# A relational graph layer on one core: three buffers for relation rows and one-hots, types brought in by transfers, and gathers that wait for their ring's slots

## The reference

```python
src, dst = (edge_index[0], edge_index[1])
m = x[src] * rel[edge_type]
m = jnp.concatenate([m[:half] @ W_in, m[half:] @ W_out], 0)
deg = jax.ops.segment_sum(jnp.ones((e,), x.dtype), dst, num_segments=n)
norm = 1.0 / jnp.maximum(deg, 1.0)
agg = jax.ops.segment_sum(m * norm[dst][:, None], dst, num_segments=n)
return jnp.tanh(agg + x @ W_loop + b)
```

## Time and profile before

| | |
|---|---|
| median of 3 runs | 2801.2 us (2800.81 to 2801.85) |
| span of the profiled execution | 3183.3 us |
| PE, PEld busy | 2759.1 us, 2587.3 us |
| DVE, ACT, POOL busy | 2303.9 us, 1865.5 us, 1952.0 us |
| granted TensorE clock, mean | 0.963 |
| moved by DMA | 312.57 MB |

### The profile page before, as it was taken

How to read it: one execution, slowest core, us unless ns; L and a number is a source line. 1 busy time by engine, 2 the same in 40 slices (tenths; PEclk the granted TensorE clock), 3 DMA queues, 4 the chain that set the end, 5 groups by cost and what they waited for, 6 DMA issues and landing times. The chain is left out here.

```text
span 3183.3 us, 55393 instructions
## 1 busy us (share of the span) xinstructions
PE 2759.1 (87%) x20688; PEld 2587.3 (81%) x20688; DVE 2303.9 (72%) x3258; ACT 1865.5 (59%) x3179; POOL 1952.0 (61%) x2129
## 2 busy tenths in 40 slices
PE   4888888888888888797888888888888887997998
PEld 3888888888888888796877887878777786997998
DVE  6777777777677777896777777777777776995665
ACT  6556665555555555585555555555555554785444
POOL 6666666666666666455666666666666664892223
PEclk9999989999999999899999999999999999998999
DMA  8333333333333333353333333333333333452221
GB/s 259 119 90 89 89 89 90 89 89 90 88 89 90 90 88 90 92 164 104 90 90 90 89 90 92 88 90 90 89 89 92 88 90 98 136 158 90 69 67 64
DMA packets 162458, 312.57 MB, mean 98 GB/s; under 512 B 34061, under 2 KB 95309, under 8 KB 162229
## 3 DMA queue, kind: packets, MB, share of 16 engines
q0 software_dynamic: 79872, 218.21, 23.8%
q1 hardware_dynamic: 81120, 89.89, 8.8%
q10 hardware_dynamic: 1237, 1.41, 0.2%
HBM read 263.90 MB, written 45.48 MB: 97 GB/s over the span
## 5 line engine op out<-in xcount | busy, mean ns | idle before, releaser
L740 PE MATMUL edge_rg<-edge_rel_hi,edge_hot 128*128 128x256 f32 x6656 | 1551.7, 293 | 86.6 <-issue 63.0
L740 PE MATMUL edge_rg<-edge_rel_lo,edge_hot 128*128 128x256 f32 x4992 | 1312.3, 289 | 60.0 <-issue 58.9
L740 PEld LDWEIGHTS edge_rg<-edge_rel_hi,edge_hot 128*128 128x128 f32 x6656 | 1219.6, 197 | 143.7 <-issue 92.2
L548 ACT ACTIVATE edge_hot<-edge_typ,minus_type 128x512 fp32r<-128x512 f32 x832 | 526.8, 685 | 935.9 <-DMA dense_prev<-emb_t 383.9
L740 PEld LDWEIGHTS edge_rg<-edge_rel_lo,edge_hot 128*128 128x128 f32 x4992 | 983.1, 197 | 70.0 <-issue 68.5
L623 DVE TENSOR_TENSOR edge_m_lo<-edge_rg,edge_m_hi 128x1024 fp32r<-128x1024 f32 x416 | 509.3, 1224 | 241.3 <-ACT edge_m_hi L541 127.7
L604 DVE TENSOR_SCALAR edge_hot<-edge_typ,type_of 128x512 fp32r<-128x512 f32 x832 | 582.3, 741 | 12.4 <-ACT edge_hot L548 8.7
L753 PE MATMUL edge_small<-edge_m_hi,edge_sel 128*128 128x258 f32 x1664 | 458.1, 306 | 96.3 <-DVE edge_m_lo L623 90.7
L530 POOL DMA_INDIRECT edge_xg<-emb,src x416 | 399.0, 959 | 225.9 <-issue 96.2
L530 POOL DMA_INDIRECT work<-h,src x416 | 400.7, 963 | 221.9 <-issue 101.9
L530 POOL DMA_INDIRECT edge_xg<-h,src x416 | 400.2, 962 | 216.2 <-issue 102.8
(11 more groups left out here) (183 smaller groups left out, 3933.9 us busy)
## 6 DMA issues: line engine op xcount, KB each, us to landing
work<-emb,src POOLq DMA_INDIRECT x416
edge_xg<-emb,src POOLq DMA_INDIRECT x416
work<-h,src POOLq DMA_INDIRECT x416
edge_xg<-h,src POOLq DMA_INDIRECT x416
set_x_rows<-in_x SPq DMA_DIRECT2D x25, 256.0 KB, 3.9
emb<-set_e_rows SPq DMA_DIRECT2D x25, 256.0 KB, 2.9
emb_t<-acc SPq DMA_DIRECT2D x5, 1280.0 KB
dense_prev<-emb_t SPq DMA_DIRECT2D x25, 256.0 KB, 2.7
```

Source lines behind the costliest of these rows:

```text
L548: act.activation(hot[:, q % 2, c], typ[q % 2][:], ACT.Abs, bias=K["minus_type"][:, c:c + 1]).then_inc(distances, 1)
L740: ins = pe.matmul(rg[q % 2][:, t, :], hot[:, q % 2, c, t * P:(t + 1) * P], part[:, c, :], start=(c == 0 and part is rel_hi), stop=(c == FULL))
```

## The change

- **Relation rows and one-hots have three buffers** (`DEPTH`, `of_three`), not two; `typ` in PSUM is given up for the third `rg`. The lists are new. DVE: message(3), one_window(3), low(3), add_window(6), one_hot(0). PE: one_window(3), relation_rows(0), and the transposes of four groups before stand in the middle of relation_rows. ACT: high(3), copy_sums(5), distance(0), one_hot(0), clear(3).
- **Types as int16 by transfers.** Setup writes the types as int16 to DRAM; SP starts two transfers a group (`load_types`): 512 types to all 128 partitions, and 128 types of each of the four tiles to a strip of 32 partitions. PE's spread matmul is gone. `dst` and `dst_rel` are int16 too.
- **The last types in strips.** The 16 last relations stand in each strip of 32 partitions (high part, low part). One one-hot of 128 elements a partition (`hot_rest`) serves the four tiles of a group; each tile has its own right side in `rel_rest`, zero outside its strip. The matmuls stay 28 a group.
- **Gathers** of group g wait for the message of group g - 4, once for four tiles.
- The copy of the node columns to DRAM is started from ACT, not SP. ACT's `high` waits for window sums of an earlier group, and the first window sums of a pair wait for the adds of the pair that held the same buffer.
- Preparation: eight transfers for the last relations (two before), some small operations more in setup and at the start of a layer; a buffer of zeros becomes one column.

```diff
+DEPTH = 3
+STRIP = P // GROUP
@@ phase_setup @@
             act.wait_ge(dst_in, 16)
+            act.copy(dst[:], dst_i[:]).then_inc(tables, 1)
             act.copy(K["dst"][:], dst_i[:]).then_inc(tables, 1)
             act.wait_ge(types_in, 16)
-            act.copy(K["typ"][0:TYPE_ROWS], types_i[0:TYPE_ROWS]).then_inc(tables, 1)
+            act.copy(types_h[0:TYPE_ROWS], types_i[0:TYPE_ROWS]).then_inc(tables, 1)
+            act.wait_ge(tables, 3)
+            act.dma_start(types_16.rearrange("(p k) -> p k", p=TYPE_ROWS), types_h[0:TYPE_ROWS]).then_inc(types_out, 16)
@@ phase_edges @@
-        hot = s.sb("hot", [P, 2, RCHUNKS, GROUP * P], F32R)
+        rel_rest = s.sb("rel_rest", [P, GROUP, DIM], F32R)
+        typ = s.sb("typ", [P, 2, GROUP * P], I16)
+        strips = s.sb("strips", [P, 2, P], I16)
+        hot = s.sb("hot", [P, DEPTH, FULL, GROUP * P], F32R)
+        hot_rest = s.sb("hot_rest", [P, DEPTH, P], F32R)
-        rg = [s.ps(f"rg{b}", [P, GROUP, DIM]) for b in range(2)]
-        typ = [s.ps(f"typ{b}", [P, GROUP * P]) for b in range(2)]
+        rg = [s.ps(f"rg{b}", [P, GROUP, DIM]) for b in range(DEPTH)]
@@ SP @@
+            def load_types(g):
+                wait_past(sp, hot_done, g - 1)
+                wait_past(sp, distances, HOT_ACT * (g - 1))
+                of_group = types[g * GROUP * P:(g + 1) * GROUP * P]
+                sp.dma_start(typ[:, g % 2], of_group.partition_broadcast(P)).then_inc(types_in[g % 2], 16)
+                sp.dma_start(strips[:, g % 2],
+                             of_group.rearrange("(t e) -> t e", t=GROUP).unsqueeze(1).to_broadcast([GROUP, STRIP, P]))\
+                    .then_inc(types_in[g % 2], 16)
@@ POOL @@
+                wait_past(pool, messages, g - 3)
                 for t in range(GROUP):
-
-                    if t < GROUP - 1:
-                        wait_past(pool, rel_tile, (GROUP - 1) * (g - 2) + t + 1)
-                    else:
-                        wait_past(pool, rel_done, g - 1)
@@ ACT @@
+                    act.wait_ge(messages, g + 1)
+                    if slot is of_three:
+                        wait_past(act, summed, g - 1)
-                over_groups(act, (0, later(distance)), (2, high), (0, later(one_hot)), (3, copy_sums), (0, clear_one))
+                over_groups(act, (3, high(of_three)), (5, copy_sums), (0, later(distance(of_three))),
+                            (0, later(one_hot(of_three))), (3, clear_one))
@@ DVE @@
-                for c in range(HOT_ACT, RCHUNKS):
-                    ins = dve.tensor_scalar(hot[:, q % 2, c], typ[q % 2][:], K["type_of"][:, c:c + 1], None,
-                                            ALU.is_equal)
+                    for c in range(HOT_ACT, FULL):
+                        dve.tensor_scalar(hot[:, slot(g, q), c], typ[:, q % 2], K["type_of"][:, c:c + 1], None,
+                                          ALU.is_equal)
+                    dve.tensor_scalar(hot_rest[:, slot(g, q)], strips[:, q % 2], K["type_of"][:, FULL:], None,
+                                      ALU.is_equal).then_inc(hot_done, 1)
-                over_groups(dve, (2, message), (2, one_window), (4, add_window), (2, low), (0, one_hot_later))
+                over_groups(dve, (3, message(of_three)), (3, one_window), (3, low(of_three)), (6, add_window),
+                            (0, later(one_hot(of_three))))
@@ PE @@
+                    for t in range(GROUP):
+                        if between and t == GROUP // 2:
+                            between(g, q, i)
+                        for c in range(FULL):
+                            for part in (rel_hi, rel_lo):
+                                pe.matmul(rg[b][:, t, :], hot[:, b, c, t * P:(t + 1) * P], part[:, c, :],
+                                          start=(c == 0 and part is rel_hi), stop=False)
+                        ins = pe.matmul(rg[b][:, t, :], hot_rest[:, b, :], rel_rest[:, t, :], start=False, stop=True)
-                over_groups(pe, (4, one_window), (2, relation_rows), (0, spread_later), (4, turn_over))
+                over_groups(pe, (3, one_window), (0, relation_rows(of_three, turn_over_before)), (4, turn_over_last))
```

More of the change, by code:

```diff
@@ L427, in over_groups, with phase_edges @@
         turn(STEPS + t // GROUPS_IN_RING, t % GROUPS_IN_RING)
-def phase_edges(nc, K, layer, nodes, rel, nodes_t, matrices):
+def phase_edges(nc, K, layer, nodes, types, rel, nodes_t, matrices):
     first = layer == 0
@@ L582, in later @@
                 return run
-            distance(0, 0, 0)
-            one_hot(0, 0, 0)
+            distance(of_two)(0, 0, 0)
+            one_hot(of_two)(0, 0, 0)
+            if first:
+                act.wait_ge(rel_in, 16 * (1 + P // REST))
+                for at in range(0, CHUNKS, 5):
+                    chunks = slice(at, at + 5)
+                    act.dma_start(nodes_t[chunks].rearrange("c p f -> p c f"),
+                                  columns(K, chunks).rearrange("p c k n -> p c (k n)")).then_inc(columns_out, 16)
             widest = act.value_load(K["span"][0:1, 0:1], min_val=0, max_val=2 * FAR)
@@ new lines, in later, with run, message, stage @@
+            def later(stage):
+                def run(g, q, i):
+                    if not isinstance(g, int) or g > 0:
+                        stage(g, q, i)
+                return run
+            def message(slot):
+                def stage(g, q, i):
+                    at = slice(GROUP * (q % 2), GROUP * (q % 2 + 1))
+                    dve.wait_ge(gathered[q], 16 * GROUP * (i + 1))
+                    dve.wait_ge(rel_done, g + 1)
+                    dve.tensor_tensor(rg[slot(g, q)][:], xg[q // 2][:, at, :], rg[slot(g, q)][:],
+                                      ALU.mult).then_inc(messages, 1)
+                return stage
```

253 lines of the change are left out of this document (134 added, 119 removed).

## The result

The changed kernel takes 2827.6 us (median of 4 runs, 2827.2 to 2832.9); the kernel before, on the same chip, 2801.0 (2800.0 to 2801.9). The ratio is 1.0098, 95% interval 1.0083 to 1.0112: **26.6 us slower**, where 2798 was forecast.

The account below looks back on a forecast made before the run. POOL's gathers, 5.00 us a turn, were taken to bound the kernel. 2801.2 + 0 (DVE, PE, ACT, types) - 6 (gathers) + 0 (gathers beside DVE) + 3 (edges) = 2798 us; own range 2775 to 2815, 8 in 10 2660 to 2870.

Parts of the forecast that it names:

- The pace: Edge stages: POOL's four gathers of 1.25 us set a 5.00 us turn; savings on DVE and PE are worth nothing.
- rival B: Edge turns: DVE and PE set the pace, gathers take 1.15 us or less; 2677 us, at best 2615; chance 0.27.
- The late signals: Profile's 376.9 us of "remote" waits: hardly in timed runs; over half vanish after the change, profiled span 2850 to 3000.
- Gathers, -6: POOL's gathers: gate opens earlier; bounds from nothing to 36 us of waiting saved, -6 us taken.
- Edges of stages, +3: Setup and layer starts: added cast, transfer, small operations and loads cost 3 us together; ACT's queue delay covered by 16 gathers.
- Gathers beside DVE's new operations, 0: Gathers beginning inside DVE's new SBUF one-hots lose what is left of them; phase fixed, none likelier, 0 us taken.
- The mean of 24 us: Gathers beside the new one-hots: mean loss 0.05 + 0.01 us a turn by chance of overlap, 24 us in all.
- Rival C: DVE's new one-hots (L638, L640) hold up POOL: 0.35 us every second turn, 72 us, giving 2873 us; chance 0.12.
- The Trainium skill's rule: DVE operations using both SBUF ports hold them throughout; GpSimd can't write DMA descriptors meanwhile; up to 0.49 us a turn.
- The 3000 us: Sum if every new DVE one-hot held up POOL wherever it fell, by the Trainium skill's rule: about 3000 us.
- Rival D: Late landings of types or gathers under the added transfers: 10 to 30 us, giving 2820 us; chance 0.08.

Follow-up runs that it names:

- x4: Kernel before, with the fourth tile's gather of each group left out from group 4 on: 2705.3 us, ratio 0.9658.
- x3: Changed kernel, with the fourth tile's gather of each group left out from group 4 on: 2578.3 us, ratio 0.9203.
- x9: Kernel before, unchanged, profiled once more: span 2804.6 us.
- x2: Kernel before with only the gathers' new gate (one wait for the message four groups before): 2798.8 us, ratio 0.9993.
- x1: Changed kernel with the copy of node columns cut in 25 pieces, one a turn from turn 4 on: 2816.1 us, ratio 1.0056.
- x6: x1 with the last 16 relation rows brought in by one transfer in place of eight: 2814.3 us, ratio 1.0051.
- x14: x6 with the third one-hot made by ACT in place of DVE: 2801.3 us, ratio 1.0004.
- x10: x1 with DVE's third one-hot written in the first three turns only: 2798.9 us, ratio 0.9995.
- x12: x6 with DVE's third one-hot as a comparison of two tensors, not with one number per partition: 2856.5 us, ratio 1.0200.

## Why the prediction was wrong

- **The pace: right.** Gathers at 1.25 us, four a turn; DVE's 4.76 to the hundredth (x4), and 4.38 to 4.45 after the change (x3), inside the 4.2 to 4.66 that were given. The savings on DVE and PE are there and worth nothing. With that, rival B is out: it needed gathers of 1.15 us.
- **The late signals: right in kind, wrong in place.** They have nothing to do with the timed runs. But the forecast of a span of 2850 to 3000 tied them to what waits on PE; x9 shows that they go without any change.
- **Gathers, -6: wrong by its size.** x2 gives 2 us, within what can't be told. The wait that the new gate takes away is 3.7 us at one place (x9), where the prediction looked for a little in every turn.
- **Edges of stages, +3: the first failed step.** It measured 11.5 + 1.8 = 13.3 (x1, x6). The prediction named one cost ("on ACT's queue the one-hots of group 1 stand behind it", "without cover it would cost up to 10") and took the cover of 16 gathers, 20 us, for enough. The cover did not hold: the gathers began at 60.80, POOL had ended its 16 gathers at 82.15, and the first message ended at 85.86. The prediction counted neither the eight loads against the cover, nor that DVE would start 4.3 us later beside the copy. And it priced the types' landing from one transfer of 8.1 us, for turns in the middle of the layer only; behind 6.5 MB they came after ten, and this second stop, 6.88 us, is the larger. The cost that it did name ended neither stop.
- **Gathers beside DVE's new operations, 0: the second failed step.** It measured 13 to 17 (x14, x10). That x14's 13.0 and the 13.3 of the edges make 26.3 of the 26.6 us only says that x14 is as fast as the kernel before; that lengthened gathers are what the 13.0 is, the sums of the traces show (12.3). How one gather is held was read correctly from two gathers: 0.56 us of the operation left, 0.44 lost, is the rule above. What failed was the sentence "paced by POOL the phase is fixed, so it is none or nearly all", by which the term became 0. In the changed kernel DVE waits for gathers in every turn, and yet the place at which its one-hots meet them wanders: 134 of 1664 gathers began inside one, and layer 0 of that trace lost 12.8 us more than x2's, layer 1 only 1.5. The mean of 24 us would have given 2822 and been nearer, but by luck: the new one-hots themselves lost 9.1 us, not 24, and another 6.2 over x2's came at the selection, which the prediction left out. The trace that it had read has 138 gathers lengthened at the selection, by 25.6 us together.
- **Rival C: the mechanism was right, the size was not.** Its 72 us came of 0.35 us lost in every second turn; in the changed kernel's trace the one-hots lengthened 53 gathers in 416 turns.
- **The Trainium skill's rule** (SBUF — State Buffer, section "SBUF: two separate sides") gives the shared pair of ports for a whole instruction to whichever of the two begins first, and the other waits. One side of it is borne out: a gather that begins second ends only after the operation does (1.43 us for 0.95 at 367.35). The other is not: a gather that begins first takes 0.94 us, and yet costs DVE 0.05 us (0.53 for 0.48). The prediction held against the rule a cast inside a gather that lost nothing; that gather was first, so by the rule too it loses nothing. The 3000 us charged every operation to POOL, which the page doesn't say. For an operation with two inputs from SBUF, as in x12, the page has the rule only against a GpSimd operation that reads SBUF; the gathers, which take their row numbers from SBUF, were held.
- **Rival D:** out but for the start. DVE's whole wait for types is 9.4 us, 5.1 of it at the one place beside the copy, and ACT's 24.6 us, 6.3 of it there.

What stays open: why the selection, 0.48 us inside SBUF in both kernels, meets so few gathers in x2 (18 began inside it, for 61 in the changed kernel) and so few again when the third one-hot goes (26 in x10); what DVE waits for at the branch, and why longer beside the copy; and how the copy's 11.5 us would divide if ACT's queue were free of it, since no run has that.

## What to carry to other kernels

Where GpSimd's indirect gathers set the pace, as here, the time of VectorE's operations inside SBUF is a cost even if VectorE idles. Don't take it for nothing because the phase looks fixed: take the mean over all phases as a size, count the old operations with the new ones, and look in the trace at hand for gathers that are already too long. Inputs in PSUM (x2) and ScalarE (x14) cost no gather anything here; shorter pieces should help by the rule, but no run tried them. A move off an engine that doesn't pace buys nothing, so ask of it only what it puts in the way of the one that does. Before a large copy is moved or anything is put ahead of it, count the whole head of the stage, loads, preparation and transfers beside the copy, against the cover, from the moment at which the cover starts to run.

## What the hardware showed that was not expected

- One profiled execution of the kernel before was 13.6% longer than its timed runs (3183.3 against 2801.2), with signals seen 4 us late; another of the same program had 2804.6. A wait of a profile whose span disagrees with the times isn't to be argued from.
- A gather that begins just after a VectorE operation inside SBUF goes first, and the operation takes 0.53 us for 0.48; one that begins later ends 0.82 us after the operation does (367.35 + 1.43 against 367.28 + 0.68). The border lay at 0.08 to 0.09 us for the comparison against a number (changed kernel) and at 0.03 to 0.04 us for that of two tensors (x12, and the selection).
- The same comparison of 512 int16 values took 495 ns against a number for each partition (x6) and 687 against that number spread along the row (x12). With 512 fp32 values from PSUM it took 742 ns in the kernel before (x2).
